# Two output rows from four transformed inputs in the third layer's 3x3 filter, the transforms split between DVE and GpSimd

## The reference

```python
def _L2_conv_ref(x, w_hidden, b_hidden, w_dw, b_dw, gamma, beta, w_out, b_out):
    ...
    hidden = _conv2d(x, w_hidden, b_hidden)                      # 1x1, 48 -> 288 channels
    qkv = _conv2d(hidden, w_dw, b_dw, groups=C6, padding='SAME') # 3x3, each channel by itself
    q, k, v = jnp.split(qkv, 3, axis=1)
    ...
    out = jnp.fft.irfft2(q_fft * k_fft, s=(PATCH, PATCH))        # q_fft, k_fft: rfft2 of 64-pixel pieces
    ...
    normed = (out - mu) / jnp.sqrt(var + EPS)                    # over the channels
    normed = normed * gamma[None, :, None, None] + beta[None, :, None, None]
    return _conv2d(v * normed, w_out, b_out)                     # 1x1, 96 -> 48 channels
```

## Time and profile before

| | |
|---|---|
| median of 3 runs | 13860.85 us (13852.76 to 13888.82) |
| the profiled execution | 13866.59 us, span 13864.8 us |
| TensorE busy over the span | 13296.2 us (96%) |
| TensorE's weight loads, beside its matmuls | 9296.9 us (67%) |
| DVE | 6964.2 us (50%) |
| ACT | 5451.2 us (39%) |
| GpSimd | 2040.2 us (15%) |

### The profile page before, as it was taken

One profiled execution on the slowest core, in us unless ns is written; L12 is line 12 of the kernel. 1 busy time (PEld: TensorE's weight loads), 2 busy tenths in 40 slices (PEclk: granted clock), 3 DMA queues, 4 the chain that ended last, 5 costly groups with the idle time before them and its releaser, 6 DMA issues. The chain is left out here.

```text
span 13864.8 us, 314775 instructions
## 1 busy us (share of the span) xinstructions
PE 13296.2 (96%) x130266; PEld 9296.9 (67%) x130266; DVE 6964.2 (50%) x15422; ACT 5451.2 (39%) x11157; POOL 2040.2 (15%) x1508
## 2 busy tenths in 40 slices
PE   7999999999899989999999999999998999999998
PEld 6877444677677765666666666666665877787877
DVE  0001777333345444444444444444445777777777
ACT  0000111211133333444444444444444676666676
POOL 0000222000000540000000000000001444333443
PEclk9999999999999999999999999999999999999999
DMA  4333665946655875444444454444443222222222
GB/s 128 134 131 109 160 161 153 163 93 135 127 154 154 215 192 56 59 56 55 58 59 55 56 58 58 55 56 58 58 55 65 51 52 53 53 52 51 53 51 48
DMA packets 2314183, 1243.88 MB, mean 90 GB/s; under 512 B 1860697, under 2 KB 2226768, under 8 KB 2233444
## 3 DMA queue, kind: packets, MB, share of 16 engines
q1 hardware_dynamic: 2045700, 1121.51, 41.8%
q10 hardware_dynamic: 267232, 104.65, 3.2%
HBM read 642.39 MB, written 450.74 MB: 79 GB/s over the span
## 5 line engine op out<-in xcount | busy, mean ns | idle before, releaser
L1526 PE MATMUL l_c<-l_wa,l_xa 128*128 128x288 f32 x12288 | 3204.9, 411 | 5.6 <-issue 5.1
L1526 PEld LDWEIGHTS l_c<-l_wa,l_xa 128*128 128x128 f32 x12288 | 2254.2, 190 | 900.1 <-issue 212.1
L1607 ACT ACTIVATE l_qkv<-l_c 128x288 f32<-128x288 f32 x2048 | 728.8, 408 | 2362.8 <-PE l_c L1530 2362.8
L1693 DVE TENSOR_TENSOR l_z<-l_f,l_ks 94x384 f32<-94x384 f32 x1024 | 566.5, 553 | 2170.5 <-ACT l_ks L1612 2170.5
L1281 PE MATMUL l1h_ps<-l1h_ring,l1h_w 96*96 96x256 f32 x6120 | 1326.6, 379 | 50.6 <-ACT l1h_ring L1229 46.9
L1052 PE MATMUL l1v_ps<-l1v_rows,l1v_w 96*96 96x256 f32 x6120 | 1326.0, 378 | 32.1 <-ACT l1v_rows L1025 32.1
L1996 PEld LDWEIGHTS l_e<-k_ident,l_turn 128*112 128x112 f32 x9900 | 1084.3, 134 | 258.4 <-issue 130.4
L1281 PEld LDWEIGHTS l1h_ps<-l1h_ring,l1h_w 96*96 96x96 f32 x6120 | 998.7, 163 | 378.4 <-issue 47.3
L1996 PE MATMUL l_e<-k_ident,l_turn 128*112 128x128 f32 x9900 | 1162.6, 276 | 92.5 <-DVE l_out L2158 86.4
L1052 PEld LDWEIGHTS l1v_ps<-l1v_rows,l1v_w 96*96 96x96 f32 x6120 | 990.5, 162 | 367.2 <-issue 31.1
L2079 ACT ACTIVATE l_spread<-l_e 112x512 f32<-112x512 f32 (+1 forms) x1584 | 860.5, 569 | 730.6 <-PE l_e L1996 709.9
(11 more groups left out here) (231 smaller groups left out, 18716.4 us busy)
## 6 DMA issues: line engine op xcount, KB each, us to landing
l0a_x<-x_px_dram SPq DMA_DIRECT2D x128, 1176.0 KB, 5.2
l0b_x<-x_in_dram SPq DMA_DIRECT2D x128, 493.8 KB
l_xa<-x_dram SPq DMA_DIRECT2D x1280, 48.0 KB, 4.0
l_xb<-l_xa SPq DMA_DIRECT2D x768, 72.0 KB
l_x<-x3p_dram SPq DMA_DIRECT2D x132, 384.0 KB
l_out<-x_dram SPq DMA_DIRECT2D x528, 96.0 KB
out_dram<-l_out SPq DMA_DIRECT2D x132, 384.0 KB
x_dram<-l0b_out ACTq DMA_DIRECT2D x256, 193.5 KB, 3.1
```

The costliest lines, as they stand in the source:

```text
L1526: nc.tensor.matmul(bank[h][:, 0:OUTC], xa[:, k, row * PW + h * 128 + dx:row * PW + h * 128 + dx + 128], wa[:, b, dx, :], start=(dx == 0), ...
L1607: nc.scalar.activation(qkv[:, j % 4, m, :], bank[m % 2][:, 0:OUTC], ACT.Copy).then_inc(conv_out, 1)
```

## The change

The 3x3 filter is computed for two rows at a time. With d0 to d3 the four input rows around a pair of output rows and g0, g1, g2 the filter's rows, four products are made: of d0 - d2 with g0, of d1 + d2 with (g0 + g1 + g2) / 2, of d2 - d1 with (g0 - g1 + g2) / 2, and of d1 - d3 with g2. Call the results m0 to m3; the first output row is m0 + m1 + m2 and the second m1 - m2 - m3. The code forms m0 + m1 and m3 - m1 and adds m2 to both, so the second row comes out with its sign turned; that cancels in the product of q and k, and for v a negated copy of `wout` undoes it.

So `filters(p, b, g)` now makes both rows of 128 columns at once: four matmuls of 128 partitions (one for each m, in banks `m0` to `m3`) and four of 20 partitions, which start at partitions 0, 32, 64 and 96 of the new tile `left`. The window's partitions now run over the three column offsets instead of the three rows: 48 channels at offset 0, 48 at 1 and 32 at 2 in the 128 partitions of `raw` and, transformed, of `pix`; the other 16 at offset 2, and ones, in `left`, once for each m.

The transforms d0 - d2 and d1 - d3 are made by DVE, the other two by GpSimd, each 128 x 516 elements for half a block, one block ahead, into `pix`:

```diff
+            def sums(n, half, i):                        # GpSimd
+                pool.wait_ge(shifted[n % NR], 48 + 48 * (n // NR))
+                if n >= 2:
+                    pool.wait_ge(conv_done, 16 * (2 * (n - 2) + half + 1))
+                d, part = planes(n, half, i)
+                in0, in1, op = ((d[1], d[2], ALU.add), (d[2], d[1], ALU.subtract))[i - 1]
+                nc.gpsimd.tensor_tensor(part, in0, in1, op).then_inc(pix_out, 1)
+            def add_second(p, j, g):                     # GpSimd
+                pool.wait_ge(m2_out, 4 * p + g + 1)
+                pool.wait_ge(m0_out, 4 * p + g + 1)
+                pool.wait_ge(m3_out, 4 * p + g + 1)
+                q = qkv[:, j % 4, 2 * g:2 * g + 2, :]
+                nc.gpsimd.tensor_tensor(q, q, copies[:, g % 2, 1:2, :].broadcast_to([128, 2, OUTC]), ALU.add)\
+                    .then_inc(qkv_out, 1)
...
+            for p in range(TOTAL + 2):
+                for g in range(4):
+                    if p < TOTAL - 2 and g % 2 == 1:
+                        sums(p // 2 + 1, p % 2, g // 2 + 1)
+                    if p < TOTAL:
+                        add_second(p, p % PAIRS, g)
+                if p % 2 == 1 and p >= 3:
+                    cut_block((p - 3) // 2)
...
-                nc.scalar.activation(qkv[:, j % 4, m, :], bank[m % 2][:, 0:OUTC], ACT.Copy).then_inc(conv_out, 1)
+                nc.scalar.activation(copies[:, g % 2, 0, :], m1[:, 0:OUTC], ACT.Copy).then_inc(m1_out, 1)
+                act.wait_ge(conv_done, 4 * n + 2)
+                if n >= 2:
+                    act.wait_ge(qkv_out, n - 1)
+                nc.scalar.activation(copies[:, g % 2, 1, :], m2[:, 0:OUTC], ACT.Copy).then_inc(m2_out, 1)
...
+            def differences(n, half, i):                 # DVE
+                ...
+                in0, in1 = (d[0], d[2]) if i == 0 else (d[1], d[3])
+                nc.vector.tensor_tensor(part, in0, in1, ALU.subtract).then_inc(diff_out, 1)
+            def add_first(p, j, g):                      # DVE
+                n = 4 * p + g
+                dve.wait_ge(m1_out, n + 1)
+                dve.wait_ge(conv_done, 4 * n + 3)
+                dve.wait_ge(t_out, 2 * p + 2)
+                nc.vector.tensor_tensor(qkv[:, j % 4, 2 * g, :], m0[:, 0:OUTC], copies[:, g % 2, 0, :], ALU.add)\
+                    .then_inc(m0_out, 1)
+                dve.wait_ge(conv_done, 4 * n + 4)
+                nc.vector.tensor_tensor(qkv[:, j % 4, 2 * g + 1, :], m3[:, 0:OUTC], copies[:, g % 2, 0, :], ALU.subtract)\
+                    .then_inc(m3_out, 1)
```

DVE's list of a turn becomes (new steps marked):

```diff
             def turn(p, j, b):                           # DVE
                 if before:
                     moments(p - 1, 0)
                     scales(p - 1, 0)
+                if now:
+                    add_first(p, j, 0)
+                if before:
                     products(p - 1, 3)
                     times_v(p - 1, j - 1, 0)
                 if now:
+                    add_first(p, j, 1)
                     products(p, 0)
-                if before:
-                    moments(p - 1, 1)
+                if ahead:
+                    differences(p // 2 + 1, p % 2, 0)
                 if last:
                     residual(p - 2, j - 2)
                 if before:
+                    moments(p - 1, 1)
+                if now:
+                    add_first(p, j, 2)
+                if before:
                     scales(p - 1, 1)
+                if now:
+                    products(p, 1)
                 if last:
                     count(p - 2, j - 2)
-                if now:
-                    products(p, 1)
                 if before:
                     times_v(p - 1, j - 1, 1)
                 if now:
+                    add_first(p, j, 3)
                     products(p, 2)
+                if ahead:
+                    differences(p // 2 + 1, p % 2, 3)
```

SP's list for a block `n`: ten loads as before, three copies that shift columns, two that keep the rows of the residual (`mid`), and twice eight into `left`, half of them from `pix` and half ones from a table `k_within`:

```diff
+            for n in range(N):
+                if n + 3 < N:
+                    load(n + 3)
+                if n + 2 < N:
+                    shift_columns(n + 2)
+                if n + 1 < N:
+                    copy_left(n + 1, 0)
+                if n >= 1:
+                    store(n - 1)
+                if n + 1 < N:
+                    copy_left(n + 1, 1)
...
+            def shift_columns(n):
+                ...
+                if n >= NX:
+                    sp.wait_ge(res_out, 3 + 2 * (n - NX) + 2)
...
+            def copy_left(n, half):
+                sp.wait_ge(pix_out, 4 * n + 2 * (half + 1))
+                sp.wait_ge(diff_out, 4 * n + 2 * (half + 1))
+                ...
+                for i in range(4):
+                    sp.dma_start(left[32 * i:32 * i + 16, n % 2, first:end - 1],
+                                 pix[HI + 32:HI + C, n % 2, i, first + 1:end]).then_inc(left_in[n % 2][half], 16)
+                    sp.dma_start(left[32 * i + 16:32 * i + 20, n % 2, first:end],
+                                 D["k_within"][i, :, (n % NBLK) * RUN + first:(n % NBLK) * RUN + end])\
+                        .then_inc(left_in[n % 2][half], 16)
```

More of the change, by code:

```diff
@@ L142, in shape_constants @@
         col[s, max(0, 1 - s):W + 1 - s] = 1
-    inside = np.zeros((5, H, PW), np.float32)
-    inside[0, 1:] = col[0]
+    image = np.zeros((3, H + 2, PW), np.float32)
     for s in range(3):
-        inside[1 + s, :H - 1] = col[s]
-    inside[4] = col[0]
-    c["k_inside"] = inside
+        image[s, 1:H + 1] = col[s]
+    first, second, third, fourth = (image[:, k:k + H:2] for k in range(4))
+    within = np.zeros((4, 4, H // 2, PW), np.float32)
+    for i, part in enumerate((first - third, second + third, third - second, second - fourth)):
+        within[i, 0:3] = part
+    within[1, 3] = 1
+    c["k_within"] = within.reshape(4, 4, H // 2 * PW)
+    gk = np.zeros((128, 3), np.float32)
+    for i, g in enumerate(((1, 0, 0), (0.5, 0.5, 0.5), (0.5, -0.5, 0.5), (0, 0, 1))):
+        gk[32 * i:32 * i + 32] = g
+    c["k_gk"] = gk
     f = np.zeros((64, 64), np.float32)
@@ L1397, in there, with planes @@
             return lag <= p < TOTAL + lag
-        def rows(tile, k, first):
-            return tile[:, k, :].rearrange("p (r w) -> p r w", w=PW)[:, first:first + 3:2, :]
+        def planes(n, half, i):
+            x = raw[:, n % NR, :].rearrange("p (r w) -> p r w", w=PW)
+            part = pix[:, n % 2, i, half * HALF:(half + 1) * HALF].rearrange("p (r w) -> p r w", w=PW)
+            return [x[:, 4 * half + k:4 * half + k + 3:2, :] for k in range(4)], part
         @block.gpsimd
@@ new lines, in copy_left @@
+            def copy_left(n, half):
+                sp.wait_ge(pix_out, 4 * n + 2 * (half + 1))
+                sp.wait_ge(diff_out, 4 * n + 2 * (half + 1))
+                first, end = half * HALF, (half + 1) * HALF
+                for i in range(4):
+                    sp.dma_start(left[32 * i:32 * i + 16, n % 2, first:end - 1],
[3 more added lines that the diff above has]
+                        .then_inc(left_in[n % 2][half], 16)
@@ L1562, in project @@
                 pe.wait_ge(turn_out, 1 + 2 * q + 2)
[L1563 to L1565 removed]
+                for s in range(2):
+                    last = nc.tensor.matmul(tp[s * 64:(s + 1) * 64, :], wout[:, s, :], tt[:, j % 2, s, :], start=True, stop=True,
                                             skip_group_check=True)
@@ L1629, in read_turned @@
                 act.wait_ge(proj_done, q + 1)
-                nc.scalar.activation(tt[:, j % 2, g, :], tr[0:C2, :], ACT.Copy).then_inc(turn_out, 1)
+                nc.scalar.activation(tt[:, j % 2, :, g * 256:(g + 1) * 256], tp[0:C2, :].rearrange("p (s x) -> p s x", s=2),
+                                     ACT.Copy).then_inc(turn_out, 1)
             def turn(p, j, b):
-                now, before, _ = (there(p, n) for n in range(3))
+                now, before, last = (there(p, n) for n in range(3))
+                if last:
+                    read_turned(p - 2, j - 2, 1)
                 if before:
```

328 lines of the change are left out of this document (168 added, 160 removed).

## The result

The changed kernel takes 13288.49 us in the median of 4 runs (13286.31 to 13299.96), the kernel before, run beside it, 13856.81 (13852.42 to 13888.82). The direction was right, the size was not.

A forecast was written before the change was run, and what follows sets the result against it. It took DVE's chain with holds, 20.4 us a turn against TensorE's 16.9, as the bound. 256 x (20.97 - 20.4) = 146 us less and 10 more gave a 13729 us span, 13730 measured; range 13330 to 14040.

The forecast's parts named there:

- TensorE after the change: TensorE's work in a turn: filters fall from 3.69 to 2.66 us each, so it needs 16.9 us a turn.
- The holds: DVE steps with two SBUF inputs wait for GpSimd on the shared port, lengthening DVE's chain from 16.2 to 20.4 us.
- The difference asks at 8.2 and ends at 9.9, not 8.9: +1.0: DVE's first difference of a turn, held by GpSimd's add_second 1, ends 1.0 us later.
- Rival (c): Holds bite less: turn 19.4 with one difference free, 18.4 with both; 13470 and 13220 us, 12830 without holds; chance 0.16.
- The sum: Whole kernel: 146 us less over 256 turns, 10 more at the start, giving a span of 13729 us.
- `times_v` ends at 7.06, not 5.75: +1.3: DVE's first times_v of a turn, held by GpSimd's add_second 0 and sums, ends 1.3 us later.
- +0.9: DVE's times_v 1 asks at 15.0 while GpSimd's add_second 2 and second sums hold until 16.1: 0.9 us more.
- DVE's list without holds: DVE's chain of dependent steps in one turn, no waits for GpSimd: 16.2 us, just below TensorE.
- rival (a): GpSimd's additions are slower, 1.57 and 1.41 us: turn 21.24, 13945 us; chance 0.18.
- Rival (b): Copies into left come late, up to 2.35 us more a turn: 14330 us at worst, 14030 at half; chance 0.09.
- Hidden, by a little.: Copies into left land by 17.8 to 19.5 us; filters want them at 18.2 and can take them 1.6 later.
- Wrong if the differences stand at 0.69: Sign in the third layer's profile: DVE's differences at their unheld 0.69 us would refute the forecast.

The follow-up runs named there:

- e1: Changed kernel with the fourth full-height matmul of each filter moved ahead of the four 20-row ones; 13165.71 us, ratio 0.9497.
- e5: Changed kernel with a one-SBUF-input statistics instruction directly ahead of each difference on DVE, at the first in the product's place; 13757.62 us, ratio 0.9923.
- e6: Changed kernel with GpSimd's two sums of a turn moved from ahead of add_second to behind it; 13310.17 us, ratio 0.9595.
- e2: Changed kernel without the 20-row matmuls, so part of the filter and the bias are missing; 13115.79 us, ratio 0.9462.
- e8: Changed kernel without the 20-row matmuls and with GpSimd's sums moved behind add_second; 12810.36 us, ratio 0.9233.
- e3: Changed kernel with all four transformed inputs made on GpSimd, one ahead of each add_second, and none on DVE; 13282.56 us, ratio 0.9581.

## Why the prediction was wrong in size, by its steps

**"TensorE after the change": mis-sized, 16.9 against 18.61.** The step took 0.52 us for a full-height matmul, 3.10 / 6 of the earlier trace rows. e1 shows that the 3.10 are six times 0.485 and 0.2 for the step down to smaller row groups. The order of the changed kernel makes that step twice in a filter: 4 x 0.485 + 2 x 0.19 + 0.70 = 3.02, where 2.66 was taken. Four 20-row matmuls side by side cost 0.70 and not the pair's 0.59, and `spectrum` 0.82 and not 0.75. Together 4 x (0.37 + 0.07) = 1.8 us a turn, and 16.9 + 1.8 = 18.7. Of these 0.44 us a filter, 0.19 are the second step down, at which the prediction did not look, 0.11 the 20-row matmuls, 0.07 `spectrum`, and only 0.06 the division of a block by its count (4 x 0.485 + 0.19 = 2.13 for 2.07). The forecast's lower bound of 0.59 for the 20-row ones was the right end to pick. Why `spectrum` is longer stays open. The Trainium skill (TensorEngine Tiling (Array Packing), Key Properties) says that changing the tiling mode, not just the tile, drains TensorE. It gives no time for it; the 0.2 us of e1 against the changed kernel agree with it, though no run here tells a drain from another cost of that change, such as the weight load.

**"The holds": the failed step, 20.4 against 17.94.** "The difference asks at 8.2 and ends at 9.9, not 8.9: +1.0", and the same again for the second: each costs nothing. The order of the starts was right (0.22 us after `add_second`, 0.24 forecast), the winner was wrong. GpSimd pays instead, 2.16 for 1.40, and nobody minds: in the whole kernel `spectrum`'s matmuls waited 0.4 us for `add_second`. Rival (c) had this as its case "both", 18.4 and 13220 us, and the earlier trace rows spoke against it: there the first to start wins, DVE by 0.08 us and GpSimd by 0.20. What DVE had in flight ahead was not looked at. In the fourth layer of the kernel before it was a copy out of PSUM (L2054): 187 times L2149 came 0.03 to 0.38 us after L2218 with this copy in flight, and each time it was held, 1.20 us or more for 0.68. Such a copy is no stand-in for a product, and no row of before has the sequence of the changed kernel. The Trainium skill (SBUF — State Buffer, Who interferes with whom) has the one that issues first keep the shared read port and the other block. The blocking agrees with the rows here: 2.16 us of `add_second` are 0.90 to the end of the difference and 1.26 more. Who wins doesn't follow from the recorded starts: in the changed kernel the later start wins, in e5 the earlier one at the same margin, and in e6 the earlier one at 0.40 us. What the runs do show is the condition: a product ahead of the difference that began 0.11 us or more before `add_second`. Whether the chip goes by the dispatch of the queued difference or by something else that a product does and a statistics instruction doesn't stays open; no run tells these apart.

**The sum.** With 18.61 in place of 20.4 the forecast's own sum is 13729 - 256 x 1.79 + 9 (for the start) = 13280; the span is 13284.5. So it is these two steps together: with the holds alone mended (17.94) and TensorE left at 16.9 the sum would have been 256 x (20.97 - 17.94) = 776 us less and some 13100, too fast. The two errors pull in opposite directions, and the wrong step set the forecast; that the direction was right says little for the mechanism, since the bound that was named was not the one that held.

**"`times_v` ends at 7.06, not 5.75: +1.3" and "+0.9": right in kind, too long.** That is 2.2 us a turn; e2 shows 2 x (1.03 - 0.56 + 0.94 - 0.56) = 1.7, in the changed kernel it is 0.9. The shift, at nothing in the forecast, adds 0.16. `sums` took 1.10 and not 1.29. These together bring the 18.4 of rival (c) to e2's 17.94: 16.2 + 1.7 + 0.16 = 18.1.

**What held.** DVE's list without holds, 16.2: e8 less the holds that it still has gives 16.1. `add_first` free at 0.45; `add_second` 1.40 when free, by the line through the earlier trace rows, which was 0.19 too high for `sums`. So rival (a), slow additions, is out. Rival (b) is out: the left copies cost TensorE 21 us in all, and their issue was 0.53 as the earlier trace rows had it for the loads; the sentence "Hidden, by a little." is right too, as e8 shows at 16.75 a turn. The 20-row matmuls run side by side. The granted clock is 1.00 in the window, the 2.4 GHz level, as before. The start was 19 us later, not 10.

**The signs named ahead.** "Wrong if the differences stand at 0.69": they do. "DVE about nine tenths busy" of 20.4 became eight tenths of 18.61, and "TensorE busy near 17 of each 20.4" became all of 18.61; this row alone, read first, shows that the bound stayed where it was.

## What to carry to other kernels

Count how often the order of issue steps from full-height matmuls down to row groups, and price that step by itself; a block of matmuls divided by its count hides it. Putting all of a kind together was worth 0.9% here. Where a forecast rests on who wins a race of 0.2 us between DVE and GpSimd for SBUF operands, both outcomes belong in the range with nearly equal chances, since the instruction in flight ahead decides with the margin. A moved instruction can move a hold and not end it: look at every group that can be held, not only at the one that was meant (e6, e3). And of two chains that are within 4% of each other (18.61 and 17.94) shortening one gains only down to the other: TensorE's order alone brought 0.5 of its 0.8 us a turn, GpSimd's order alone brought nothing, and on top of TensorE's it brought some 70 us more.

## What the runs showed of the chip that was not expected

The step from 128-row matmuls down to 20-row ones in four row groups, or to 64-row ones, costs about 0.2 us of TensorE's time, with 288 columns of fp32 and a clock of 1.00. Four such 20-row matmuls side by side take 0.70 us, with the way back in it whatever that costs; a 128-row one takes 0.485.

A DVE subtraction with both inputs in SBUF, started 0.22 us after a GpSimd addition, took its free 0.68 us while the addition grew from 1.40 to 2.16; with a statistics instruction in place of the product ahead of it on DVE, at 0.21 us, it was held to 1.75. With the product ahead, it went free when the product had begun 0.11 us or more before the addition, and was held at 0.08 or less. The product without a difference behind it held nothing (e3). A DVE instruction of four elements a partition can be held as well: 1.58 us for 0.16.

Two-input additions on GpSimd took 1.10 us for 516 elements (1.098 in the median) and 1.40 for 576: the 60 elements between them are not worth 0.3 us by the slope of the earlier trace rows, so the shape of the operands (the second of `add_second`'s is one row read twice) counts too; that wasn't tried by itself.
